# A kernel of layer norm, recurrent mixer and routed experts: where the copies of transposed x, the moments, one x transfer and the diagonals stand

## What is computed

```python
xn = layernorm(x)                       # per token: (x - mean) / sqrt(var + 1e-5)
out = x + attn(xn) + ffn(xn)

# attn: causal depthwise convolution of 4 taps, two gates, a linear recurrence
c = conv(xn) + conv_b
r, i = sigmoid(c @ W_r.T + b_r), sigmoid(c @ W_i.T + b_i)
a = sigmoid(log_a) ** (8 * r)
h[t] = a[t] * h[t-1] + sqrt(max(1 - a*a, 0))[t] * (i * c)[t]
attn = rmsnorm(h @ W_out.T) * gamma

# ffn: each token goes to the one best of 8 experts, at most 512 tokens per expert
probs = softmax(xn @ Wr); e = argmax(probs)
rank = number of earlier tokens with the same expert; kept if rank < 512
ffn = relu(xn @ W1[e]) @ W2[e] * probs[e]    # 0 for tokens that are not kept
```

## Time and profile before

| | us |
|---|---|
| median of 3 runs | 131.7 (131.4 to 132.49) |
| the profiled execution, its own time | 131.36 |
| its span, first to last instruction | 129.6 |
| busy: PE / PEld | 105.8 / 86.2 |
| busy: DVE / ACT / POOL | 97.5 / 91.2 / 82.4 |

### The profile page before, as it was taken

One profiled execution on the slowest core, in us unless ns is written; L12 is line 12 of the kernel. 1 busy time (PEld: TensorE's weight loads), 2 busy tenths in 40 slices (PEclk: granted clock), 3 DMA queues, 4 the chain that ended last, 5 costly groups with the idle time before them and its releaser, 6 DMA issues.

```text
span 129.6 us, 2078 instructions
## 1 busy us (share of the span) xinstructions
PE 105.8 (82%) x676; PEld 86.2 (67%) x676; DVE 97.5 (75%) x217; ACT 91.2 (70%) x209; POOL 82.4 (64%) x107
## 2 busy tenths in 40 slices
PE   4999898999798999999999999999999996300000
PEld 4998797753377758838937989999699895200000
DVE  6388888989899990290098269999998959975870
ACT  2467598945688479969968999969971896903730
POOL 8966794038787877777787877777878877500000
PEclk9999999999999999999999999999999999855555
DMA  2994994962354362512451441111211111149996
GB/s 64 321 290 77 351 387 191 401 277 58 67 202 119 130 197 71 197 41 54 76 199 41 89 175 53 53 61 41 61 46 61 43 53 51 61 123 321 334 336 181
DMA packets 14346, 19.27 MB, mean 149 GB/s; under 512 B 1664, under 2 KB 10112, under 8 KB 14336
## 3 DMA queue, kind: packets, MB, share of 16 engines
q1 hardware_dynamic: 7952, 12.65, 30.4%
q0 software_dynamic: 2048, 4.20, 10.8%
q10 hardware_dynamic: 4336, 2.30, 6.7%
HBM read 10.76 MB, written 8.39 MB: 148 GB/s over the span
## 4 chain that ended last, share of the span: by engine, by line
PE 48%; DVE 15%; DMA 14%; ACT 8%; issue 4%; POOL 4%; SPq 2%; POOLq 1%; DVEq 1%; ACTq 0%
PE bank L561 14%; PE bank L495 7%; DMA x_tok<-in_x 7%; DVE xc L940 6%; PE bank L548 5%; PE bank L550 4%; PE bank L549 4%; DMA dec<-y_rows 4%; ACT sq L723 3%; PE bank L577 3%; PE bank L535 3%; POOL xn_tok L387 2%; PE bank L427 2%; DMA xn_tok<-xn_rows,idx_in 2%; DMA y_rows<-xn_tok,idx_out 2%
## 5 line engine op out<-in xcount | busy, mean ns | idle before, releaser
L387 POOL DMA_INDIRECT xn_tok<-xn_rows,idx_in x32 | 33.4, 1042 | 16.4 <-issue 9.5
L394 POOL DMA_INDIRECT y_rows<-xn_tok,idx_out x32 | 32.1, 1002 | 10.1 <-issue 9.8
L561 PE MATMUL bank<-w_raw,h_sb 128*128 128x128 f32 x256 | 29.9, 275 | 0.0
L561 PEld LDWEIGHTS bank<-w_raw,h_sb 128*128 128x128 f32 x256 | 29.2, 192 | 0.0
L709 ACT ACTIVATE h_sb<-bank 128x512 f32<-128x512 f32 x32 | 18.9, 597 | 4.9 <-PE bank L550 2.8
L495 PE MATMUL bank<-xc,par 128*128 128x512 f32 x32 | 15.5, 603 | 0.0
L548 PE MATMUL bank<-xg_hi,w_split 128*128 128x512 f32 x32 | 14.4, 450 | 0.3 <-ACT h_sb L709 0.3
L914 DVE TENSOR_TENSOR w_split<-w_raw,w_split 128x512 fp32r<-128x512 f32 x8 | 5.5, 683 | 11.5 <-ACT w_split L654 11.5
L550 PE MATMUL bank<-xg_hi,w_split 128*128 128x512 f32 x32 | 12.6, 394 | 0.0
L549 PE MATMUL bank<-xg_lo,w_split 128*128 128x512 f32 x32 | 12.5, 391 | 0.0
L940 DVE SCALAR_TENSOR_TENSOR xc<-xnT,par,xc 128x1020 f32<-128x1020 f32 (+2 forms) x9 | 11.5, 1278 | 0.3
(11 more groups left out here) (118 smaller groups left out, 204.1 us busy)
## 6 DMA issues: line engine op xcount, KB each, us to landing
w_raw<-in_weights SPq DMA_DIRECT2D x8, 512.0 KB, 3.6
y_rows<-sca SPq DMA_DIRECT2D x4, 512.0 KB, 5.5
dec<-y_rows SPq DMA_DIRECT2D x8, 256.0 KB, 5.2
xn_rows<-xn_tok SPq DMA_DIRECT2D x3, 512.0 KB, 4.4
x_tok<-in_x ACTq DMA_DIRECT2D x2, 512.0 KB, 7.8
out<-dec SPq DMA_DIRECT2D x4, 256.0 KB, 3.6
out<-dec ACTq DMA_DIRECT2D x4, 256.0 KB, 3.5
x_tok<-in_x SPq DMA_DIRECT2D x2, 256.0 KB, 4.3
```

Source lines behind the costliest of these rows:

```text
L387: g.indirect_dma_start(gathered[:, s * D:(s + 1) * D], None, xn_rows, bass.IndirectOffsetOnAxis(ap=idx_in[:, s:s + 1], axis=0)).then_inc(g ...
L394: g.indirect_dma_start(y_rows, bass.IndirectOffsetOnAxis(ap=idx_out[:, s:s + 1], axis=0), gathered[:, s * D:(s + 1) * D], None).then_inc(s ...
L561: last = mm(tile_of(e, s), h_sb[:, k * CAP + s * P:k * CAP + (s + 1) * P], w_raw[:, e, F + k * D:F + (k + 1) * D], start=(k == 0), stop=(k ...
```

## The change

The change has four parts.

1. x is loaded by six transfers in place of five (LOADS). Unit 3 comes in two transfers of four tiles, both issued by SP, each with a semaphore of its own. TensorE waits for a transfer at the half that begins with it; VectorE waits in the middle of `moments(3)` for the second of them. The transfers that ACT issues are the same as before (the numbers are now 2 and 5).
2. All eight raw halves are copied by ACT, in order. Halves 3 and 5 leave VectorE. On ACT the copies of halves 3 and 5 are put in; half 6 stands ahead of root(4), and `normalise(2)` and half 4 ahead of root(3). `transposed` waits on one semaphore.
3. VectorE does moments(3) and moments(4) one after the other, then inverse(3). inverse(4) comes after the first group of the marks.
4. POOL makes the diagonals after `normalise(4)` in place of before it.

```diff
@@ -164,7 +164,10 @@
         UNITS = ((0, 4), (4, 4), (8, 8), (16, 8), (24, 8))
         NU = len(UNITS)
 
-        x_in = [sem(f"x_in{u}") for u in range(NU)]
+        LOADS = ((0, 4), (4, 4), (8, 8), (16, 4), (20, 4), (24, 8))
+        NL = len(LOADS)
+
+        x_in = [sem(f"x_in{m}") for m in range(NL)]
         par_in = sem("par_in")
         gam_in = sem("gam_in")
         w_in = [sem(f"w_in{e}") for e in range(E)]
@@ -191,7 +194,6 @@
         router_w = sem("router_w")
         tp_done = sem("tp_done")
         xT_act = sem("xT_act")
-        xT_dve = sem("xT_dve")
         xn_tp = sem("xn_tp")
         xnT_done = sem("xnT_done")
         logits_done = sem("logits_done")
@@ -248,9 +250,7 @@
         POOL_TILES = (2, 3, 6, 7, 9, 10, 11, 14, 15, 17, 18, 19, 22, 23, 25, 26, 27, 30, 31)
         ACT_TILES = (0, 1, 4, 5, 8, 12, 13, 16, 20, 21, 24, 28, 29)
 
-        DVE_HALVES = (3, 5)
-
-        ACT_UNITS = (2, 4)
+        ACT_LOADS = (2, 5)
         PE_CONV = 2
 
         def normalised(eng, n):
@@ -260,10 +260,7 @@
                     eng.wait_ge(done, count)
 
         def transposed(eng, n):
-            if n in DVE_HALVES:
-                eng.wait_ge(xT_dve, sum(m <= n for m in DVE_HALVES))
-            else:
-                eng.wait_ge(xT_act, n + 1 - sum(m <= n for m in DVE_HALVES))
+            eng.wait_ge(xT_act, n + 1)
 
         def convolved(eng, n):
 
@@ -303,12 +300,12 @@
 
         @block.sync
         def _(sp):
-            for u, (t0, nt) in enumerate(UNITS):
-                if u not in ACT_UNITS:
-                    sp.dma_start(tiles(x_tok, t0, nt), tile_rows(x_rows, t0, nt)).then_inc(x_in[u], 16)
-
-            for u in range(NU):
-                sp.wait_ge(x_in[u], 16)
+            for m, (t0, nt) in enumerate(LOADS):
+                if m not in ACT_LOADS:
+                    sp.dma_start(tiles(x_tok, t0, nt), tile_rows(x_rows, t0, nt)).then_inc(x_in[m], 16)
+
+            for m in range(NL):
+                sp.wait_ge(x_in[m], 16)
             for e in range(2):
                 sp.dma_start(w_raw[:, e, :], weights[:, e * WW:(e + 1) * WW]).then_inc(w_in[e], 16)
             sp.dma_start(gam[:, :], gamma.partition_broadcast(P)).then_inc(gam_in, 16)
@@ -375,12 +372,12 @@
             normalise(1)
             normalise(2)
             normalise(3)
+            normalise(4)
             pool.wait_ge(par_in, 16)
             pool.wait_ge(ident_done, 1)
             for k in range(TAPS):
                 g.tensor_scalar(diag[:, k, :], ident[:, :], par[:, CONV_W + k:CONV_W + k + 1], 0.0, ALU.mult,
                                 ALU.add).then_inc(diag_done, 1)
-            normalise(4)
 
             def gather(e):
                 for s in range(e * ST, (e + 1) * ST):
@@ -429,9 +426,9 @@
                 last.then_inc(logits_done, 1)
 
             for n in range(NH):
-                for u, (t0, nt) in enumerate(UNITS):
+                for m, (t0, nt) in enumerate(LOADS):
                     if t0 == 4 * n:
-                        pe.wait_ge(x_in[u], 16)
+                        pe.wait_ge(x_in[m], 16)
                 if n >= 2:
                     transposed(pe, n - 2)
                 for i in range(4):
@@ -599,9 +596,9 @@
         def _(act):
             a = nc.scalar.activation
             act.dma_start(par[:, :], params).then_inc(par_in, 16)
-            for u in ACT_UNITS:
-                t0, nt = UNITS[u]
-                act.dma_start(tiles(x_tok, t0, nt), tile_rows(x_rows, t0, nt)).then_inc(x_in[u], 16)
+            for m in ACT_LOADS:
+                t0, nt = LOADS[m]
+                act.dma_start(tiles(x_tok, t0, nt), tile_rows(x_rows, t0, nt)).then_inc(x_in[m], 16)
             nc.scalar.preload_act_table_set("sqrt_and_others")
 
             def root(u):
@@ -636,11 +633,13 @@
             untile(2)
             root(2)
             normalise(1)
+            untile(3)
             untile(4)
+            normalise(2)
             root(3)
-            normalise(2)
+            untile(5)
+            untile(6)
             root(4)
-            untile(6)
             untile(7)
             normalise(3)
             normalise(4)
@@ -787,8 +786,10 @@
 
             def moments(u):
                 t0, nt = UNITS[u]
-                dve.wait_ge(x_in[u], 16)
                 for t in range(t0, t0 + nt, 2):
+                    for m, (l0, _) in enumerate(LOADS):
+                        if l0 == t:
+                            dve.wait_ge(x_in[m], 16)
 
                     v.bn_stats(stats[:, t:t + 2, :].rearrange("p t c -> p (t c)"),
                                x_tok[:, t * D:(t + 2) * D].rearrange("p (j d) -> p d j", j=2)
@@ -802,10 +803,6 @@
                 dve.wait_ge(rstd_done, u + 1)
                 v.scalar_tensor_tensor(nmr[:, cols], stats[:, cols, 1], -1.0, rstd[:, cols], ALU.mult,
                                        ALU.mult).then_inc(nmr_done, 1)
-
-            def untile(n):
-                dve.wait_ge(tp_done, n + 1)
-                v.tensor_copy(xT[:, n * HT:(n + 1) * HT], tp[n % 2][:, :]).then_inc(xT_dve, 1)
 
             moments(0)
             dve.wait_ge(centre_mm, 1)
@@ -817,13 +814,10 @@
             moments(1)
             inverse(1)
             moments(2)
-            untile(3)
             inverse(2)
             moments(3)
-            untile(5)
+            moments(4)
             inverse(3)
-            moments(4)
-            inverse(4)
 
             results = [0]
 
@@ -854,6 +848,8 @@
                 v.scalar_tensor_tensor(onehot[:, :, t], nth[:, t, :].rearrange("p t e -> p e t"), 1.0,
                                        eq[:, t, :].rearrange("p t e -> p e t"), ALU.is_equal,
                                        ALU.mult).then_inc(onehot_done, 1)
+                if n0 == 0:
+                    inverse(4)
             dve.wait_ge(onehot_done, len(MARKED))
             v.tensor_tensor_scan(run[:, :, :].rearrange("p e t -> p (e t)"),
                                  tmask[:, :, :].rearrange("p e t -> p (e t)"),
```

## The result

Over 20 runs of each kernel the changed one took 130.91 us (129.84 to 131.48), the one before 131.59 us (130.93 to 132.49). The ratio is 0.994, with a 95% interval of 0.9921 to 0.9959: 0.8 us faster, 0.5 to 1.0. The forecast was 0.53 us faster and no change beyond 1%. Two more sets of 12 runs of the changed kernel gave 130.99 and 130.91 us (0.9944 and 0.9941).

A forecast was written before the change was run, and what follows sets the result against it. One chain of waits through TensorE's router matmuls to the table and gathers bounds the kernel. Waits of 0.36 and 0.83 us go, 0.69 comes, overlap aside 0.53 gained: 131.7 to 131.2 us, range 130.4 to 132.2.

The forecast's parts named there:

- The sum: Whole kernel: waits of 0.36 and 0.83 us go, one of 0.69 us comes; 0.53 us gained, bounds 0.3 to 0.7.
- The new wait at router(3): TensorE before router(3): idle 0.69 us for half 3, which ACT copies only after root(2) and normalise(1).
- the first half of unit 3: x load: lands near 8.4 us, bounds 8.4 to 10.8; TensorE wants it at 10.39.
- The split: x's unit 3: removes TensorE's wait of 0.36 to 0.44 us; landing late at 10.8 would cost under 0.1 us.
- The order of ACT: ACT's copies before the last router matmuls: slack 0.37 us for half 5, 0.45 for half 6; router(7) starts at 16.43.
- The diagonals: POOL, after normalise(4): ready at 20.7 us, at the latest 22.3; TensorE wants them at 21.7, so cover 1.0 us.
- inverse(4): VectorE, behind the first marks: ends at 16.6 instead of 16.05 us; normalise(4) loses at most 0.5 us, which is covered.
- A sign that was drawn too narrow: Expert stage: prediction wrong if the span from first gather to end changes by more than 0.5 us.
- rival 1: After the marks: POOL holds VectorE up for two diagonals, 0.8 us, giving 132.0 us; chance 0.1.
- rival 2: Head: ACT's copies, roots and tiles become the bound, gain only 0 to 0.2 us, 131.5 to 131.7; chance 0.12.
- rival 3: Convolution: late diagonals on POOL delay table and gathers, up to 3.1 us, giving 134.3 us; chance 0.06.
- rival 4: Gathers: y_rows zeroing and last store begin 1.6 us earlier, half of it comes through, giving 130.4 us; chance 0.1.

The follow-up runs named there:

- the third profile: One profiled execution of the unmodified changed kernel, from its second repeat set; that set measured 0.9941 of the kernel before.
- the first profile: One profiled execution of the unmodified changed kernel, from its original set of 20 runs; 131.15 us, the set 0.994 of the kernel before.
- the second: One profiled execution of the unmodified changed kernel, from its first repeat set; that set measured 0.9944 of the kernel before.
- the closer order: Changed kernel with ACT copying half 3 right after root(2) and half 5 right after root(3), normalise(1) and normalise(2) later; 0.991 of the kernel before.
- both parts undone: Changed kernel with unit 3 as one transfer again and the diagonals before normalise(4) again; 131.0 us, 0.9947 of the kernel before.
- the first edit: Kernel before with ACT's copy of half 6 moved ahead of root(4), nothing else; 1.0013 of the kernel before.
- the second edit: Kernel before with half 6 ahead of root(4), plus inverse(4) moved behind the first marks on VectorE; 0.9921 of the kernel before.

## Why the prediction was right

*The sum.* Forecast 0.53 us, measured 0.8 (0.5 to 1.0). The steps agree best in the third profile, whose start (6.42) is that of before (6.38): free at 17.41 against a forecast of 17.32, second marks 17.73 against 17.63. The whole mechanism, that TensorE's wait for half 6 goes, that one for half 3 comes, and that the balance is passed to the end, is shown by the waits and by the last scatter, 0.79 us earlier in the first profile and 0.47 in the third. What lies between 0.5 and 0.8 in the medians I can't assign; the start of the head varies by 0.9 us among the profiles, and the forecast lies at the lower edge of the interval. The prediction held that a difference under 1% can't be told from none; over 20 runs of each kernel 0.6% was told from none.

*The new wait at router(3)* was forecast at 0.69 us; it was 0.50 in the first profile, about 0.15 in the second (transposes 4 at 10.47, router(3) at 11.06, less the usual 0.44) and 0.27 in the third. This is the term that was mis-sized. I held ACT's root(2) at 9.94, but it hangs on VectorE's moments and these on the start, and TensorE's arrival hangs on other things. It is still the largest idle time from router(3) on, and the closer order that takes it away has 0.4 us less by the ratios, as it should, within intervals that overlap. The second mis-sized term is small: the first half of unit 3 was estimated to land near 8.4 and landed near 9.1, still before TensorE wanted it.

*The split* was costed at under 0.1 us because something else is late: shown by the waits of the profile without it (free at 17.36) and by the time with both parts undone; the time without the split alone (0.9971) speaks against it and is not explained. *The order of ACT* was given a slack of 0.37 and more for halves 5 and 6: no wait in front of R5, R6 or R7 in any profile of the changed kernel. *The diagonals* were forecast ready at 20.7 and wanted at 21.7; it was 20.44 and 21.43. *inverse(4)* behind the marks was covered as said. *A sign that was drawn too narrow*: the span from the first gather to the end was to change by no more than 0.5 us. It is 102.0 us before and 102.4, 101.9 and 101.3 us in the three profiles of the change, so by the third alone the prediction would count as wrong, through the spread of the last reads of y_rows.

*What I had not seen*: I took the moved copies for the cause of the gain, since they had made root(4) late. They may be one way to cure it: without them the moments of unit 4 end at 13.11 instead of 15.2. No kernel here moves the copies and leaves half 6 behind root(4), so that this alone would do is argued and not shown. Letting half 6 pass root(4) is a way that is shown, and needs inverse(4) moved as well.

*The rivals.* POOL holding VectorE up (rival 1) did not eat the gain. From the second marks to idx_in it is 8.38 us before and 8.33 to 8.37 in the three profiles of the change. In the other kernels it is up to 8.71, so POOL beside VectorE may be worth 0.3 us there; no experiment isolated that. By the Trainium skill's rule on the port pair ("SBUF — State Buffer", "SBUF: two separate sides") an instruction of POOL that reads SBUF stands still while a VectorE instruction with two SBUF inputs holds it. The diagonal of 1.45 us beside VectorE's f16 work, with a median of 0.43 in the changed kernel, agrees in kind; VectorE's own comparisons took 2.67 us against 2.49. ACT as the bound (rival 2) was seen only as the wait at router(3). The late diagonals (rival 3) exist as a mechanism, with a far steeper price than I gave. The earlier zeroing (rival 4) left no mark: from the first gather to the first read of y_rows it is 86.2 us before and in the first profile of the change.

## What to carry over

In a chain of engines that each work in a fixed order, look for an instruction that stands behind another one's late input, and check at once which engine is the next to be late. Here the first edit alone took away TensorE's wait of 0.8 us, VectorE became the late one, and nothing was gained; the second edit freed it. A part that gains nothing today (the split transfer, by its profile) may be worth 0.4 us once the wait behind it is gone, so retry it after each step. When a change is under 1%, follow the shift stage by stage, since the span of one execution carries half a microsecond of other spread at each end.

## What the runs showed of the hardware that I had not expected

- TensorE, idle for 4.0 us in the middle of a busy program, came back at a granted clock of 0.55 to 0.59, and f32 taps took 0.86 us instead of 0.43. In the window from 30 to 32 us it was granted 1.00 again. This added about 1.5 us (6.6 less 5.0) to a stall of 4.2 us.
- A GpSimd tensor_scalar on 128x128 values took 0.37 us when undisturbed and up to 1.45 us beside VectorE's f16 products and comparisons, which together lost 0.2 us (0.74 and 2.67 us against 0.69 and 2.49).
- The start of TensorE's chain differs by 0.9 us among executions of the same head (5.73 to 6.64 us for the first copy), while the granted clock reads 1.00 from 4 to 7 us in the six of these profiles that were read there.
- The last reads of y_rows took between 3.46 and 6.28 us in the chains of one and the same kernel.
